# A four-layer transformer in one kernel: the last tile's steps, stores per tile, and another order of work in the third layer

## The reference

```python
xn = _layernorm(x, axis=-1)
s = _L0_attn_ref(xn, ...)          # one attention per layer
g = _silu(_L0_ffn_ref(xn, ...))    # one feed-forward network per layer
x = x + s * g
```

## Time and profile before

| | us |
|---|---|
| median of 3 runs | 4606.95 (4597.4, 4606.95, 4609.44) |
| the profiled execution | 4609.57 |
| its span | 4607.8 |
| layer 0 | 0 to 640 |
| layer 1 | 641 to 2817 |
| layer 2 | 2817 to 3548 |
| layer 3, positions | 3548 to 3890 |
| layer 3, sets | 3890 to 4592 |
| store | 4592.9 to 4607.8 |

### The profile page before, as it was taken

The page is one execution under the profiler, slowest core; times in us unless marked ns, Lnnn a source line. Parts: engine busy times, 40 slices in busy tenths (PEclk is TensorE's granted clock), DMA queues, the critical chain, the costliest instruction groups (busy, mean ns, idle before and its releaser), DMA issues. The chain is left out here.

```text
span 4607.8 us, 56275 instructions
## 1 busy us (share of the span) xinstructions
PE 4409.5 (96%) x19733; PEld 2574.6 (56%) x19733; DVE 2500.0 (54%) x5812; ACT 1684.7 (37%) x3240; POOL 202.4 (4%) x324
## 2 busy tenths in 40 slices
PE   7999999999999999999999999999998898999997
PEld 3444446766666676666667665666565454333332
DVE  6666653252524325252432534887888787666664
ACT  3444442232232323223232324444443221455554
POOL 0222200000000000000000000000000000000000
PEclk9999999999999999999999999999998998999999
DMA  3011012111121211112121111000000000110011
GB/s 85 13 18 36 16 46 73 74 65 66 64 81 64 83 73 65 66 64 81 64 83 73 64 66 51 1 1 1 0 1 20 0 1 21 18 18 15 15 20 40
DMA packets 51043, 196.47 MB, mean 43 GB/s; under 512 B 9656, under 2 KB 19264, under 8 KB 33608
## 3 DMA queue, kind: packets, MB, share of 16 engines
q1 hardware_dynamic: 49968, 192.84, 12.8%
q10 hardware_dynamic: 816, 0.20, 0.0%
HBM read 169.54 MB, written 4.33 MB: 38 GB/s over the span
## 5 line engine op out<-in xcount | busy, mean ns | idle before, releaser
L1114 PE MATMUL l_exp_out<-l_w,l_hidden 128*128 128x256 f32 x4096 | 905.2, 381 | 0.4
L1104 PE MATMUL l_hid<-l_xn_t,l_w 128*128 128x512 f32 x2048 | 891.1, 593 | 0.0
L1114 PEld LDWEIGHTS l_exp_out<-l_w,l_hidden 128*128 128x128 f32 x4096 | 774.1, 190 | 118.9 <-issue 9.0
L1228 ACT ACTIVATE l_hidden<-l_hid,l_w 128x512 f32<-128x512 f32 x512 | 351.3, 686 | 930.5 <-PE l_hid L1104 930.5
L1104 PEld LDWEIGHTS l_hid<-l_xn_t,l_w 128*128 128x128 f32 x2048 | 388.9, 190 | 466.4 <-issue 453.6
L484 DVE TENSOR_REDUCE l3f_row_max<-l3f_bank 128x1 f32<-128x512 f32 x512 | 328.1, 685 | 184.7 <-PE l3f_bank L367 184.2
L1395 DVE SCALAR_TENSOR_TENSOR l_moe<-l_exp_out,l_gates,l_moe 128x256 f32<-128x256 f32 x256 | 123.7, 483 | 449.1 <-PE l_exp_out L1114 443.4
L440 ACT ACTIVATE l3f_prob_t<-l3f_bank 128x512 f32<-128x512 f32 x512 | 278.1, 596 | 230.8 <-PE l3f_bank L374 230.6
L374 PE MATMUL l3f_bank<-l3f_qk_t 32*128 32x512 f32 x1024 | 312.3, 637 | 3.7 <-ACT l3f_prob_t L440 2.5
L481 DVE CUSTOM_DVE_ANT_0 l_masked<-l_bank,l_mask 128x256 f32<-128x256 f32 (+3 forms) x512 | 226.7, 487 | 157.3 <-PE l_bank L367 156.3
L367 PE MATMUL l3f_bank<-l3f_qk_t 32*128 32x512 f32 x1024 | 302.0, 657 | 6.0 <-DMA l3f_qk_t<-l3f_packed 5.2
(11 more groups left out here) (446 smaller groups left out, 6099.2 us busy)
## 6 DMA issues: line engine op xcount, KB each, us to landing
l_w<-in_w SPq DMA_DIRECT2D x128, 1024.0 KB, 4.9
l_mix<-l_cum SPq DMA_DIRECT2D x32, 512.0 KB, 3.8
l_qk_t<-l_packed SPq DMA_DIRECT2D x128, 64.0 KB
l3f_qk_t<-l3f_packed SPq DMA_DIRECT2D x128, 64.0 KB
all_x<-in_x SPq DMA_DIRECT2D x8, 512.0 KB, 6.2
out_x<-all_x SPq DMA_DIRECT2D x8, 512.0 KB, 5.7
l_hidden<-in_fp4w SPq DMA_DIRECT2D x1, 2304.0 KB
l_qk_t<-l_max_rows SPq DMA_DIRECT2D x128, 2.0 KB
```

What stands on the lines that cost most here:

```text
L1104: ins = nc.tensor.matmul(bank[:, :], w1[:, e % 2, c, f * P:(f + 1) * P], xn_t[:, c, :], start=c == 0, stop=c == CT - 1)
L1114: ins = nc.tensor.matmul(bank[:, 0:C], hidden[:, e % 2, f, j * P:(j + 1) * P], w2[:, e % 2, f, :], start=f == 0, stop=f == HF - 1)
L1228: hid.empty(nc.scalar.activation(hidden[:, e % 2, f, :], bank[:, :], ACT.Relu, bias=w[:, B1][:, e * HF + f:e * HF + f + 1]), (e, f))
```

## The change

1. `Attention.tensor`: in the steps with no scores left (w >= ALL), the transposed scores of heads 2 and 3 are issued right behind those of heads 0 and 1, before the values, in banks of the ring "score". The pass at the end of the step is left out there.
2. `layer3_sets`: the last tile has steps of its own. Its output is made by halves (two banks, each started with the bias by a matmul of one row), its y is transposed by channel halves, tanh, the products and the addition into x run per half; `s_all` is halved beforehand.
3. Stores: tile b - 2 is stored at step 2 of tile b, the last in two halves, from SyncE inside layer 3; `store` goes.
4. Layer 2: the transposes of xq and their copies become a function `rounded_in`. It runs ahead of `normal_in` in tiles 2 to 6, right after the scores at TURN, and ahead of hidden_out at LAST. At TURN the numerator comes before hidden_out(3); DVE there does gated before hidden_product and the denominator between start_x and finish_x. In tile 6 DVE does denominator and attention_out before finish_h. At the start ACT copies the first queries and keys before it splits the weights, and DVE makes the features before start_weight(0).

```diff
@@ class Attention, def tensor @@
-            bank = flow.open(pe, "score_t", ("t", t, s))
+            bank = flow.open(pe, "score" if w >= n and s >= HPG // 2 else "score_t", ("t", t, s))
...
             score_t(0)
             score_t(1)
+            if w >= n:
+                score_t(2)
+                score_t(3)
...
-        if 0 <= t < n:
+        if 0 <= t < n and w < n:
             score_t(2)
             score_t(3)
@@ def layer2, tensor @@
-            def gate_up(t):
+            def rounded_in(t):
                 fx.wait_restored(pe, t + 1)
...
+            def gate_up(t):
...
                 score(t)
+                if t == TURN:
+                    rounded_in(t - 1)
                 if t < LAST:
                     query_key(t + 1)
                 if t == TURN:
                     gate_up(t - 1)
+                    numerator(t)
                     hidden_out(t - 2)
                 elif t == LAST:
+                    rounded_in(t)
                     hidden_out(t - 2)
                     gate_up(t)
-                numerator(t)
+                if t != TURN:
+                    numerator(t)
...
-                if t + 2 < B:
+                if t == 1:
                     normal_in(t + 2)
-                if t == 1:
                     weights_in()
+                    rounded_in(0)
                     gate_up(0)
                     down_in()
-                elif 1 < t < TURN:
-                    gate_up(t - 1)
-                    hidden_out(t - 2)
-                elif t == TURN:
-                    gate_up(t)
-                    hidden_out(t - 1)
-                elif TURN < t < LAST:
-                    gate_up(t)
+                elif 1 < t < LAST:
+                    rounded_in(t if t >= TURN else t - 1)
+                    if t + 2 < B:
+                        normal_in(t + 2)
+                    gate_up(t if t >= TURN else t - 1)
+                    if t <= TURN:
+                        hidden_out(t - 1 if t == TURN else t - 2)
@@ def layer2, scalar (the same order of calls as TensorE's, and at the start) @@
+            act.wait_ge(bias_loaded, 16)
+            query_key(0, 0)
             act.wait_ge(fp4_loaded, 16)
             fh.split(weight(0), weight(0), weight_lo(0))
-            act.wait_ge(bias_loaded, 16)
-            query_key(0, 0)
-            fh.split(weight(1), weight(1), weight_lo(1))
             value(0)
             normal_in(1)
+            fh.split(weight(1), weight(1), weight_lo(1))
@@ def layer2, vector @@
-            start_weight(0)
             features(0, 0)
             features(0, 1)
+            start_weight(0)
...
             finish_h(t - 2)
+            gated(t - 3)
             hidden_product(t - 1)
-            gated(t - 3)
             start_x(t)
+            denominator(t)
             finish_x()
             start_h(t - 1)
-            denominator(t)
...
-                finish_h(t - 1)
                 denominator(t)
                 attention_out(t)
+                finish_h(t - 1)
@@ def layer3_sets, tensor @@
+            def output(b):
+                banks = [flow.open(pe, "score", ("p", b, half)) for half in range(2)]
+                parts = [banks[j // 2][:, j % 2 * C:(j % 2 + 1) * C] for j in range(TJ)]
+                for bank in banks:
+                    nc.tensor.matmul(bank[:, :].rearrange("p (j c) -> p j c", c=C), cst[0:1, C_ONES:C_ONES + P],
+                                     w[0:1, BP].unsqueeze(1).to_broadcast([1, 2, C]), start=True, stop=False)
+                pe.wait_ge(y_ready, b + 2)
+                transposes(("yt", b, 1), lambda j: y[:, j, P:C])
+                flow.wait_emptied(pe, ("yt", b, 0))
+                for j in range(TJ):
+                    nc.tensor.matmul(parts[j], y_t[:, 0, j * P:(j + 1) * P], wp[:, 0, :], start=False, stop=False)
+                flow.wait_emptied(pe, ("yt", b, 1))
+                for j in range(TJ):
+                    ins = nc.tensor.matmul(parts[j], y_t[:, 1, j * P:(j + 1) * P], wp[:, 1, :], start=False, stop=j % 2 == 1)
+                    if j % 2:
+                        flow.fill(ins, ("p", b, j // 2))
...
+                elif b == B - 1:
+                    if i == 2:
+                        pe.wait_ge(y_ready, b + 1)
+                        transposes(("yt", b, 0), lambda j: y[:, j, 0:P])
+                    elif i == 4:
+                        output(b)
@@ def layer3_sets, sync @@
+                if i == STORE and b >= 2:
+                    sp.wait_ge(gate_used, b - 1)
+                    sp.dma_start(token_rows(b - 2), x_all[:, b - 2]).then_inc(stored, 16)
+            for half in range(2):
+                js = slice(2 * half, 2 * half + 2)
+                sp.wait_ge(gate_used, B + half)
+                sp.dma_start(token_rows(B - 1)[:, js], x_all[:, B - 1, js]).then_inc(stored, 16)
+            sp.wait_ge(stored, 16 * (B + 1))
@@ def layer3_sets, scalar @@
+                elif i == 10 and b == B - 1:
+                    act.wait_ge(gate_used, b)
+                    for half in range(2):
+                        bank = flow.wait_filled(act, ("p", b, half))
+                        nc.scalar.activation(gate[:, 2 * half:2 * half + 2, :].rearrange("p j c -> p (j c)"), bank[:, :], ACT.Tanh,
+                                             scale=0.5).then_inc(tanh_ready, 1)
@@ def layer3_sets, vector (last tile; y by channel halves at steps 1 and 2) @@
+                    elif i == 3:
+                        st.link(V.tensor_scalar(s_all[:, b], s_all[:, b], 0.5, None, ALU.mult))
+                    elif i in (10, 11):
+                        half = i - 10
+                        js = slice(2 * half, 2 * half + 2)
+                        bank = flow.wait_filled(dve, ("p", b, half))
+                        dve.wait_ge(tanh_ready, b + 1 + half)
+                        flow.empty(V.tensor_tensor(out[:, js, :], bank[:, :].rearrange("p (j c) -> p j c", c=C), s_all[:, b, js], ALU.mult),
+                                   ("p", b, half))
+                        flow.wait_emptied(dve, ("p", b, half))
+                        st.link(V.scalar_tensor_tensor(gate[:, js, :], gate[:, js, :], 1.0, out[:, js, :], ALU.add, ALU.mult))
+                        V.tensor_tensor(x_all[:, b, js], x_all[:, b, js], gate[:, js, :], ALU.add).then_inc(gate_used, 1)
...
-                if i == 6 and b >= 1:
+                if i == 6 and 1 <= b < B:
                     flow.wait_filled(dve, ("yt", b - 1, CT - 1))
```

More of the change, by code:

```diff
@@ L915, in _ @@
                     ahead.norm.normalise(nc, dve, 0, st, lambda j: x_all[:, 0, j, :])
[L918 to L928, removed]
 SN, SH, SP_ = 16, 8, 64
@@ L1866, in down_in, with rounded_in, gate_up @@
                     copy_out(("down", m), down_t[:, 2 * m:2 * m + 2, :].rearrange("p a n -> p (a n)"), 2 * C)
-            def gate_up(t, features):
+            def rounded_in(t):
                 for c in range(CT):
                     copy_out(("xq", t, c), xq_t[:, c, :], T)
+            def gate_up(t, features):
                 act.wait_ge(phi_ready, 2 * features)
@@ L1932, in _ @@
                     split_rows(t, 3)
-                if t + 2 < B:
+                if t == 1:
                     normal_in(t + 2)
-                if t == 1:
                     weights_in()
+                    rounded_in(0)
                     gate_up(0, t + 2)
                     down_in()
-                elif 1 < t < TURN:
-                    gate_up(t - 1, t + 2)
-                    hidden_out(t - 2)
-                elif t == TURN:
-                    gate_up(t, t + 2)
-                    hidden_out(t - 1)
-                elif TURN < t < LAST:
-                    gate_up(t, t + 2)
+                elif 1 < t < LAST:
+                    rounded_in(t if t >= TURN else t - 1)
+                    if t + 2 < B:
+                        normal_in(t + 2)
+                    gate_up(t if t >= TURN else t - 1, t + 2)
+                    if t <= TURN:
+                        hidden_out(t - 1 if t == TURN else t - 2)
+                elif t + 2 < B:
+                    normal_in(t + 2)
             hidden_out(LAST - 1)
@@ L2677, in _, with layer3_sets @@
                     extremes_in()
-def layer3_sets(nc, w_dram, l3c, x_all, s_all, meanvar, rstd, set_q, set_k, cst):
+def layer3_sets(nc, w_dram, l3c, x_all, s_all, meanvar, rstd, set_q, set_k, cst, out_dram):
     (WQ, WK, WV, WP, BP), width = spans(*L3F_SIZES)
@@ L3012, in layer3 @@
         layer3_positions(nc, wa_dram, dora_dram, c_dram, x_all, s_all, sim, norms, l3c, set_q, set_k, cst)
-        layer3_sets(nc, wf_dram, l3c, x_all, s_all, norms.meanvar, norms.rstd, set_q, set_k, cst)
+        layer3_sets(nc, wf_dram, l3c, x_all, s_all, norms.meanvar, norms.rstd, set_q, set_k, cst, out_dram)
 def build(nc, d, out):
@@ L3026, in build @@
         layer2(nc, d["l2w"], d["fp4w"], x_all, cst, norms)
-        layer3(nc, d["l3a"], d["dora"], d["l3c"], d["l3f"], x_all, cst, norms)
```

(2 more changed lines are left out.)

17 lines of the change are left out of this document (15 added, 2 removed).

## The result

The changed kernel takes 4566.84 us (median of 4 runs, 4563.96 to 4572.1) against 4608.19 (4 runs, 4597.4 to 4610.44): a ratio of 0.9918, 95% interval 0.9906 to 0.9929, so 41 us or 0.9% less. Its profiled execution took 4563.96 us, its span is 4562.2, its mean granted clock 0.981. Later runs, with the kernel before at 4604 and the changed one at 4565.32, gave 0.9917 (0.9904 to 0.9931).

A forecast was written before the change was run, and what follows sets the result against it. TensorE, busy 96% of the span, was taken as the bound. Layer 0's tail -7.5, layer 2 -4.6 and layer 3 -21 gave -33: 4576.5 us profiled, median 4574, range 4558 to 4590.

The forecast's parts named there:

- Tails: Last eight attention steps of layers 0 and 3: merged score passes save 7.5 us and 9.4 us.
- rival B: Layer 2: no wait for den at TURN, low-clock stretches gone, -12; in all -41, 4566 or lower; chance 0.17.
- Rival C: Tails do not shorten, ScalarE or the shared ring of four sets the step; 4583 to 4590; chance 0.16.
- End and store: Layer 3, last values to the end: last tile by halves, seven stores issued earlier; -11.9 us.
- Rival D: Layer 3: stores disturb the q/k moves, slower, 4623 at 7 us a tile; chance 0.02.
- Layer 2: Sum of start, tiles 2 to 4, tile 5 and tiles 6 and 7: -4.6 us, from -12 to +2.
- The two waits forecast for tile 5: Layer 2: TensorE waits 5 us for den's bank in hidden_out(3); start_h(4) begins at 3309.9, not 3301.2.
- The start: Layer 2's start: queries first removes the k_t wait and low clock, 3.9 + 1.7, less 0.4: -5.2 us.
- tiles 2 to 4: Layer 2: xn transposes cover the 1.50 us wait for xq_t before gate_up, 0.9 each: -2.7 us.
- TURN: Layer 2, tile 5: the 6.2 us wait is filled, but a den bank wait delays hidden_out(3): +6 us.
- tile 6: Layer 2: denominator and attention_out ahead of finish_h remove the 2.8 us l_den wait and its low clock: -2.7 us.
- what follows, I give it nothing: Layer 2, after tile 6's removed wait: the rest ends with DVE's rounding of the last tile; 0 us.

The follow-up runs named there:

- e12_three_banks: The changed kernel with all four transposed scores of a tail step in the ring of three banks; 4599.3 us, 0.9992 to the kernel before.
- e11_no_early_stores: The changed kernel with the output of tiles 0 to 6 left out; 4565.72 us, 0.9922 to the kernel before.
- a1_after: The changed kernel run again unaltered, beside more runs of the kernel before; 4565.32 us against 4604.09, 0.9917.
- e5_den_early: The changed kernel with DVE's denominator at TURN right behind gated, before hidden_product and start_x; 4559.39 us, 0.9905 to the kernel before.

## Why the prediction was right, and where it was not

The forecast was 4574 in 4558 to 4590; 4567 was measured. Tails, end and store were right in mechanism and nearly in size. That the total of the profiles without the slow clock (35 for 33) came out so close is in part luck: the 4.2 us that layer 2 did not give were made up by 2.2 at the end, 2.2 in the positions and 1.4 in the sets, of which the last two were not foreseen. The medians' 41 us are the number of rival B (4566), and that is luck altogether: B's condition, no wait for l_den and 12 us from layer 2, did not come. The parts of the sum:

- **Tails.** Right in size in both layers (-7.1 for -7.5, -9.8 for -9.4), and the rows of the steady state gave the right price of a merged pass; the 3.07 times for four row tiles of the Trainium skill ("TensorE: Matmul & The Clock Gate", "Measured speedup vs the span model"), which spoke against it, isn't seen here: four heads together take 1.14 us (4519.95), one head alone 1.12 (4557.85 in e12_three_banks), both at a clock of 1.00, so four row tiles give 3.9 times. Rival C, that ScalarE or the banks set the step, was wrong for this version, but for the two steps above, and right with three banks for the pass: there e12_three_banks loses the gain of the tails and more.
- **End and store.** -14.1 for -11.9. The chain was right; what was too long were two terms of the sum: 3.0 us for the landing of the last half, which took 2.1, and 2.5 for the block's end, which took 1.4 (4560.8 to 4562.2). Rival D, stores disturbing the moves, is excluded by e11_no_early_stores. That transfers of all queues interleave on the same 16 engines (Trainium skill, "DMA: Bandwidth & Descriptors", "Issuing engines are not separate DMA queues") cost nothing at this distance.
- **Layer 2.** The two waits forecast for tile 5 came: 5.5 for l_den (5 forecast), and start_h(4) later by 9.5 relative to score(5) (8.7). The failed step is the last term of the sum. The layer gave -0.4 for -4.6. The start gave -3.6 for -5.2, tiles 2 to 4 -4.6 for -2.7, TURN +8.1 for +6 and tile 6 -4.7 for -2.7; these misses cancel. What is left is "what follows, I give it nothing": from score(7) on 4.5 us are given back. hidden_out(5) stood before gate_up(7) in the old order too, so it is not that. TensorE reaches score(7) earlier against DVE, whose rounding of tile 6's hidden values begins 12.5 us behind score(7) and not 10.6; on ScalarE the two copies of xq now go first behind split_h(6), so that hidden_out(5) waits 3.3 us and not 1.3 and runs at a low clock after it (4.66 us for 3.02); tile 7's output comes late by this, and DVE waits 1.6 us more for it. For this step there is the comparison of the traces and no experiment. TensorE in before, beside 3439.14 above:

```profile
3448.32 3.02 PE L1658 MATMUL l_bank<-l_down_t,l_hq_t 128*128 128x256 f32 x12 [1.30 <-ACT l_hq_t L1817]
```

The terms of single tiles are no more certain than 1.7 us. The value products (16 instructions) take 7.0 to 7.1 us in some tiles and 8.8 in others, at a lower clock (0.80 in the 8.8 at 2919.9), and which tiles have the 8.8 differs between two profiles of the same kernel: in the profile after the change tile 1 has it and tile 0 not, in a1_after the other way round. So it can't be said that the low clock of the start moved there. The whole layer takes 736.7 to 736.9 us in the three profiles with the old order and 734.9 to 736.8 in the seven with the new one.
- **Not in the forecast.** The slow clock at the sets' start of the profiled execution of before, 10.6 us, and 2.2 to 3.8 in the positions. Without the first the profiled difference is 35 us, and the forecast was 33. That slow clock comes in milder forms in executions of several kernels, with and without products added. Layer 1, which nothing here edits, differs too: 2171.2 to 2171.3 us in the profiles of a1_after, e5_den_early and e11_no_early_stores, 2175.8 to 2176.1 in the other ten. Whether such stretches are rarer with the change is open: 38.8 and 41.4 were measured between medians, 33 to 35 follow from the stages.

## What to carry to other kernels

A merged pass needs as many free banks as it has parts; count them before the engine's time. With a round-robin ring, list for each bank what is opened a whole turn later: a small result that its reader empties late holds up unrelated work, and a line moved up on the reader (the denominator here) can be worth more than the wait shows: here 10 to 11 us for a wait of 5.5. Compare stages and their granted clock before medians; stretches that no edit touches differed here by 5 to 14 us between executions. Transfers of finished tiles belong under the work of the next ones, one at a time.

## What the runs showed of the hardware

A wait of TensorE can cost more than its length: behind the 5.5 us wait, twelve products took 5.57 us instead of 2.95. It need not: waits of 0.7 us in e12_three_banks were followed by products at full clock in some steps and at a low one in others. A low clock can last through nearly full work: 0.59 over 38 us with TensorE busy for 36.3 in one execution, 0.88 over the same products in seven others. Four row groups of 32 rows take no longer than one (1.14 us and 1.12). And a 512 KB transfer that is alone lands in 3.0 us; among eight in a row its landing takes 5.7.
